# A gated delta rule whose transposes move to VectorE, with part of the output projection issued in its last slot

## The reference

```python
x = x + L0_attn(layernorm(x))            # x: 4 x 512 x 512; gated delta rule, 16 key heads, 32 value heads of 128
x = x + L0_xattn(layernorm(x), ctx, ctx) # 4 heads of 128, all of it dense
x = x + L0_ffn(layernorm(x))             # 512 -> 1280 -> 512, ternary weights

# L0_attn
mixed = silu(causal_conv1d(h @ w_qkv)); z = h @ w_z
q, k = l2norm(q), l2norm(k); beta = sigmoid(h @ w_b); g = -exp(A_log) * softplus(h @ w_a + dt_bias)
for t: S = S * exp(g_t); S += k_t (x) (v_t - k_t S) * beta_t; o_t = q_t S
core = rmsnorm(core) * norm_weight * silu(z)
return core.reshape(B, S, 4096) @ w_out
```

## Time and profile before

| | |
|---|---|
| median of 3 runs | 3666.68 us (3666.51 to 3670.01) |
| the profiled execution | 3667.28 us, of which its span 3665.5 us |
| PE busy | 3487.7 us (95%) |
| DVE busy | 2314.8 us (63%) |
| ACT busy | 1369.4 us (37%) |
| POOL busy | 1520.7 us (41%) |
| mean granted PE clock | 0.977 |
| largest group | L618, the projection tiles, 1424.5 us of PE |

### The profile page before, as it was taken

The page is one execution under the profiler, slowest core; times in us unless marked ns, Lnnn a source line. Parts: engine busy times, 40 slices in busy tenths (PEclk is TensorE's granted clock), DMA queues, the critical chain, the costliest instruction groups (busy, mean ns, idle before and its releaser), DMA issues. The chain is left out here.

```text
span 3665.5 us, 67720 instructions
## 1 busy us (share of the span) xinstructions
PE 3487.7 (95%) x23472; PEld 2207.6 (60%) x23472; DVE 2314.8 (63%) x4006; ACT 1369.4 (37%) x4187; POOL 1520.7 (41%) x1473
## 2 busy tenths in 40 slices
PE   4799999999999999999999999999996999999999
PEld 4466666666666666666666666666664444455444
DVE  4587777877778777878778777778772000014453
ACT  1344444444444444444444444444441000011232
POOL 0455554555545455555554555545551000001032
PEclk7999999999999999999999999999997999999999
DMA  1111111111111111111121111111104232311001
GB/s 55 44 36 30 42 42 37 30 36 44 34 36 30 36 32 51 30 36 36 31 48 30 36 30 41 43 37 30 36 24 157 87 115 69 103 58 69 1 9 38
DMA packets 94404, 165.88 MB, mean 45 GB/s; under 512 B 7841, under 2 KB 40737, under 8 KB 92449
## 3 DMA queue, kind: packets, MB, share of 16 engines
q1 hardware_dynamic: 93440, 152.47, 14.4%
q10 hardware_dynamic: 576, 8.39, 0.6%
HBM read 122.83 MB, written 38.01 MB: 44 GB/s over the span
## 5 line engine op out<-in xcount | busy, mean ns | idle before, releaser
L618 PE MATMUL d_ring<-xT,d_w 128*128 128x512 f32 x3072 | 1424.5, 607 | 12.0 <-DMA d_w<-in_w 11.6
L618 PEld LDWEIGHTS d_ring<-xT,d_w 128*128 128x128 f32 x3072 | 574.7, 194 | 585.6 <-issue 567.2
L890 DVE SCALAR_TENSOR_TENSOR d_conv<-d_ring,d_w,d_conv 128x511 f32<-128x511 f32 (+2 forms) x768 | 570.7, 743 | 287.2 <-ACT d_conv L1082 282.4
L1384 PE MATMUL t_acc<-t_area 128*128 128x512 f32 x1024 | 444.8, 595 | 18.4 <-DMA t_area<-core_rows 18.4
L1082 ACT ACTIVATE d_conv<-d_ring,d_w 128x512 f32<-128x512 f32 x256 | 176.5, 689 | 599.3 <-PE d_ring L618 599.3
L1384 PEld LDWEIGHTS t_acc<-t_area 128*128 128x128 f32 x1024 | 194.5, 191 | 256.7 <-issue 237.9
L923 DVE TENSOR_TENSOR d_zm<-d_tz,cons 128x512 f16<-128x512 f32 x384 | 264.2, 688 | 118.9 <-PE d_tz L688 114.5
L559 POOL TENSOR_TENSOR d_imd<-cons,d_dm 128x512 f16<-128x512 f32 x128 | 148.4, 1160 | 434.5 <-ACT d_dm L1133 434.5
L1613 DVE TENSOR_TENSOR t_x<-t_acc,t_x 128x512 f32<-128x512 f32 x16 | 11.1, 692 | 419.5 <-PE t_acc L1384 419.5
L511 POOL TENSOR_TENSOR d_rkt<-d_kss,cons 128x4 f32<-128x4 f32 x64 | 12.9, 201 | 610.9 <-ACT d_junk L1100 610.9
L933 DVE TENSOR_TENSOR d_em<-d_te,d_em 128x512 f16<-128x512 f32 x384 | 262.1, 683 | 4.5 <-PE d_td L697 0.2
(11 more groups left out here) (223 smaller groups left out, 6791.1 us busy)
## 6 DMA issues: line engine op xcount, KB each, us to landing
d_decay<-decay_rows SPq DMA_DIRECT2D x64, 512.0 KB, 6.1
core_rows<-d_core SPq DMA_DIRECT2D x64, 512.0 KB, 3.3
t_area<-core_rows SPq DMA_DIRECT2D x32, 1024.0 KB, 5.5
d_w<-in_w SPq DMA_DIRECT2D x96, 256.0 KB, 2.8
t_area<-in_wout ACTq DMA_DIRECT2D x2, 3072.0 KB, 21.3
ln_x<-in_x SPq DMA_DIRECT2D x16, 256.0 KB, 5.1
t_x<-in_x SPq DMA_DIRECT2D x4, 1024.0 KB, 9.9
t_area<-in_ctx SPq DMA_DIRECT2D x4, 1024.0 KB, 7.5
```

What stands on the lines that cost most here:

```text
L618: last = nc.tensor.matmul(bank(TILE[j])[:, :], wtile(j, k), xT[:, k, r % B * S:(r % B + 1) * S], start=k == 0, stop=k == KT - 1)
L890: nc.vector.scalar_tensor_tensor(c[:, d:S], bank(TILE[j])[:, 0:S - d], tap(j, KS - 1 - d), c[:, d:S], ALU.mult, ALU.add).then_inc(taps, 1)
L1384: return nc.tensor.matmul(acc[t][:, :], core[(grp * CHUNKS + q) % 3][:, t, h * P:(h + 1) * P], w[:, head, :], start=head == 0, stop=head = ...
```

## The change

1. Levels 0 to 3 no longer compute E on PE. DVE turns D into E by one instruction, `nc.vector.transpose` of 128 x 1024 fp16 in blocks of 32x32, after each of the levels 0 to 3 (`flip_d`), and E into the first D at the start (`flip_e0`). `turn_e0` and `copy_d0` go; `level_e` stays at levels 4 and 5.
2. `normal_k` moves from DVE to ACT (four instructions instead of one). `p_full` moves from DVE to POOL and reads a copy that ACT makes (`copy_kq`). The two copies of chunk 0 move from DVE to ACT (`first_state`, `first_output`).
3. The orders of all engines in a slot, the ring's order and banks, and the lags are new. v1's tile now comes after v0's.
4. `xT` and four PSUM banks `acc` (the ring and `td`) live on through `tail`. SP loads the core rows of heads 0 to 7 for group 0, and `w_out` of these heads, into columns of `xT` that are no longer needed. PE issues 24 of the 32 products on them in 19 places of the last slot and the other 8 at the start of `tail`; the output projection then starts at chunk 2. The loads of core rows and weights in `tail` are cut and ordered anew.

```diff
+EARLY = 24
@@ SP
+            sp.wait_ge(z_projected, GV * (ITERS - 1))
+            sp.wait_ge(stored, 16 * (ITERS - 4))
+            for q, b in ((0, 1), (1, 0)):
+                sp.dma_start(xT[:, :, b * S:(b + 1) * S], core_rows[0:NC, :, q * S:(q + 1) * S].rearrange("t p n -> p t n")).then_inc(early[0], 16)
+            sp.dma_start(xT[:, :, 2 * S:3 * S], wout[:, 0:KT, :]).then_inc(early[0], 16)
             slot((ROUNDS, 0), False, True, True)
+            sp.wait_ge(z_projected, GV * ITERS)
+            sp.dma_start(xT[:, :, 3 * S:4 * S], wout[:, KT:2 * KT, :]).then_inc(early[1], 16)
             slot((ROUNDS, 1), False, False, True)
@@ POOL
+            def p_full(m, h):
+                pool.wait_ge(kqs_ready, count(m))
+                pool.wait_ge(gamc_ready, nth(m, "gamc_ready", h))
+                nc.gpsimd.tensor_tensor(pT[m[1] % 2][h][:, :], kqs[:, :], gamc[m[1] % 2][h][:, :], ALU.mult).then_inc(p_ready, 1)
@@ PE
-            def turn_e0(m, h):
...
             def level_d(m, l):
                 pe.wait_ge(z_ready, at(m, LEVELS, l + 1))
-                if l:
-                    pe.wait_ge(e_added, at(m, LEVELS, l))
+                elif l < 5:
+                    pe.wait_ge(flipped, at(m, 5, l + 1))
...
+            def head_start(n, i):
+                if isinstance(n[0], int) and n == (ROUNDS, 1):
+                    if i == 0:
+                        pe.wait_ge(early[0], 48)
+                        pe.wait_ge(vn_ready, GV * ITERS)
+                        pe.wait_ge(z_silued, GV * ITERS)
+                        pe.wait_ge(zr_ready, GV * ITERS)
+                    for piece in range(EARLY * i // 19, EARLY * (i + 1) // 19):
+                        if piece == 4 * KT:
+                            pe.wait_ge(early[1], 16)
+                        early_product(nc, acc, xT, piece)
@@ DVE
+            def flip_e0(m):
+                dve.wait_ge(e0_ready, at(m, 2 * GV, 2 * GV))
+                nc.vector.transpose(dm[:, :], em[m[1] % 2][:, :]).then_inc(flipped, 1)
+
+            def flip_d(m, l):
+                dve.wait_ge(d_added, at(m, 4, l + 1))
+                nc.vector.transpose(em[m[1] % 2][:, :], dm[:, :]).then_inc(flipped, 1)
@@ ACT
+            def normal_k(n):
...
+                for c in range(NC):
+                    nc.scalar.activation(chunk(khat[n[1] % 2], c), chunk(bank("k_turn"), c), ACT.Copy, scale=rk[:, c:c + 1]).then_inc(khat_ready, 1)
+            def copy_kq(m):
...
+                nc.scalar.activation(kqs[:, :], bank("kq")[:, :], ACT.Copy).then_inc(kqs_ready, 1)
+            def first_state(s):
+                act.wait_ge(s_done, at(s, 3, 1))
+                nc.scalar.activation(state[:, :], psa[:, 0:GV * P], ACT.Copy).then_inc(first_ready, 1)
+            def first_output(s):
+                act.wait_ge(o_done, at(s, NC, 1))
+                nc.scalar.activation(oo[:, :, 0, :], psb[:, 0:GV * P].rearrange("p (h d) -> p h d", h=GV), ACT.Copy).then_inc(first_ready, 1)
@@ tail
+def early_product(nc, acc, xT, piece):
+    head, t = piece // 4, piece % 4
+    core = xT[:, t, (1 - head // 4) * S + head % 4 * P:(1 - head // 4) * S + (head % 4 + 1) * P]
+    return nc.tensor.matmul(acc[t][:, :], core, early_weights(xT, head), start=head == 0, stop=False)
-        PARTS = (0, 2, 8, 20, HV)
+        PARTS = (8, 12, 16, 24, HV)
...
+            for piece in range(EARLY, 8 * KT):
+                early_product(nc, acc, xT, piece)
             for grp in range(B):
-                for q in range(CHUNKS - 2):
+                for q in range(0 if grp else 2, CHUNKS - 2):
...
             for i in range(4):
+                if i:
+                    act.wait_ge(core_loaded[i - 1], 16)
                 act.dma_start(w[:, PARTS[i]:PARTS[i + 1], :], a["wout"][:, PARTS[i]:PARTS[i + 1], :]).then_inc(w_loaded[i], 16)
```

More of the change, by code:

```diff
@@ L424, in conv_of, with free @@
             return cb[CONV_BUFFER[name]]
-        def free(eng, n, name, order, place, freed):
-            slot_, v = back(n, -(name in LAGGED)), order.index(name)
+        def free(eng, n, name, order, place, freed, lag):
+            slot_, v = back(n, -lag[name]), order.index(name)
             for _ in range(3 * len(order)):
@@ L666, in _ @@
             PIECES = [(h, c) for h in range(GV) for c in range(NC)]
-            def turn_e0(m, h):
[L669 to L676, removed]
-                    last = nc.tensor.matmul(chunk((tz, td)[h], c), piece(em[m[1] % 2], h, c), id16[:, :], start=True, stop=True)
-                last.then_inc(a_done, 1)
             def level_z(m, l):
                 if l == 0:
-                    pe.wait_ge(d0_ready, at(m, GV, GV))
+                    pe.wait_ge(flipped, at(m, 5, 1))
+                    wait(pe, tt_ready, nth(m, "tt_ready", 1, 1))
                 elif l < 5:
@@ L822, in slot @@
                 if recur:
-                    solve(s, 2)
-                if invert:
-                    level_e(m, 2)
-                if recur:
-                    read_q(s, 2)
+                    attend(s, 1)
+                    head_start(n, 7)
+                    read_k(s, 2)
+                    head_start(n, 8)
+                if project:
+                    khat_turn(n)
                 if invert:
@@ L847, in slot @@
                 if recur:
-                    solve(s, 3)
-                if project:
-                    kk(n)
+                    attend(s, 2)
+                    head_start(n, 12)
+                    read_k(s, 3)
+                    head_start(n, 13)
                 if invert:
@@ L871, in slot @@
                 if recur:
+                    solve(s, 3)
+                    head_start(n, 15)
+                if invert:
+                    level_z(m, 5)
+                    v_turn(m, 1)
+                if recur:
+                    attend(s, 3)
+                    head_start(n, 16)
+                if invert:
+                    level_d(m, 5)
+                    level_e(m, 5)
+                if project:
+                    tile(n, 3)
+                if invert:
+                    refine(m, 1)
+                    refine(m, 0)
+                    tile(m, 4)
+                    close(m, 0)
+                if recur:
+                    o_turn(s, 0)
+                    head_start(n, 17)
                     o_turn(s, 1)
+                    head_start(n, 18)
                 if invert:
-                    close(m, 0)
                     close(m, 1)
+                    v_turn(m, 0)
             slots(pe, slot)
@@ L1110, in q_square @@
                 wait(act, eq_ready, count(n, 1))
-                squares(bank("q_turn"), NC, qss, q_squares, scale=(RMS_EPS * HD) ** 0.5)
+                wait(act, k_squares, at(n, NC, NC))
+                squares(bank("q_turn"), 0, qss, q_squares, scale=(RMS_EPS * HD) ** 0.5)
             def copy_kT(n):
```

445 lines of the change are left out of this document (222 added, 223 removed).

## The result

The changed kernel takes 3542.18 us in the median of four runs (3536.55 to 3546.47), beside 3667.24 us for the kernel before: a ratio of 0.9657, with an interval of 0.9640 to 0.9673. It is 3.4% faster, 125 us. The forecast was 3567 us with a range down to 3545, so the sign and the cause are as forecast, and the gain is 25 us larger than forecast and 3 us larger than the range allowed. The profiled execution is the slowest of the four, 3546.47 us, with a span of 3544.6 us.

What follows compares the result with a forecast made beforehand. PE was taken to bound the delta rule. From 3667.28 us: -86.8 for PE work removed, +9 for waits, -1.3 for slot 1, -21 at the end, giving 3567 us; range 3545 to 3612.

Steps and rivals of the forecast that it cites:

- The bound: Delta rule: PE is the bound, its groups following without a gap, so only work taken from PE shortens the 40.14 us slot.
- Together 1.40 us of PE in a slot: Four `level_e` (0.95 us) and two unit-matrix turns (0.46) leave PE; slot 38.74 us, 86.8 us less over 62 slots.
- The unknown price: One DVE 32x32 block transpose of 128 x 1024 fp16, shown in no row: taken as 1.21 us, bounds 0.68 and 2.66.
- The booked waits: PE's waits at six tight places in a slot: 0.15 us a slot, 9 us in all, between 0 and 0.6 a slot.
- The draining slots and slot 1: Slots without all three parts: slot 1 gives 1.3 us, the first draining slot 0, within 2 us either way.
- The end: Last slot and tail: +12 for early products, -27.8 for 32 products gone, -5 for an earlier tail start; sum -21 us.
- The turns: Hardware loop's turn of a round: PE waits 3.3 us, 12 times, taken as the loop's price and left as is.
- the lists don't mesh: Rival, chance 0.20: several tight places short by 0.3 or more, 0.5 to 1.0 us a slot lost, 3590 to 3620 us.
- DVE becomes the bound: Rival, chance 0.07: transposes at the scan's pace make DVE set the slot, 3780 us; decides from 2.2 us a transpose.
- The slots did shorten: Answers a rival, chance 0.05: POOL or ACT paces the slot at 40 us, only the end's -21 is left, 3646 us.
- the end did give: Answers a rival without its own chance: early products at half clock throughout, +21 us in the last slot, 3588 us.

Runs made afterwards that it cites:

- The first two experiments: Changed kernel plus 32 unread PE products a slot, in four groups of eight: behind each level's `level_d`, 3599.12 us; between fp32 groups, 3627.16 us.
- the second experiment: Changed kernel plus four groups of eight unread fp16 products on PE, each standing between fp32 groups: 3627.16 us, ratio 0.9902.
- the fourth experiment: Changed kernel with the DVE transposes (`flip_d`) of levels 0 to 3 each done twice: 3670.66 us, ratio 1.0022 to the kernel before.

## Why the prediction was near, and where it was short

**The bound.** Right: PE was the bound in the delta rule and still is, and what left PE's list left the slot. The first two experiments show it by putting it back.

**The slot: the step that failed.** "Together 1.40 us of PE in a slot" was too small: what left PE's list was worth 1.60 (fp16 groups 1.38, the fp32 groups behind them 0.22). I took the durations of the removed groups, 0.24 and 0.23, but put at nothing what they did to the fp32 groups behind them. Such a group takes up to 0.08 us longer behind fp16, and the second experiment makes four such places and pays 0.08 for each. Summed by distances between starts in a regular slot of either kernel:

| us of a slot | before | after |
|---|---|---|
| fp32 groups, each as long as behind fp32 | 32.93 | 32.93 |
| fp16 groups | 6.02 | 4.64 |
| what fp32 groups take longer behind fp16 | 1.18 (16 places) | 0.96 (15 places) |
| late starts at `level_d` 4 and `attend` 3 | 0 | 0.10 |
| sum | 40.13 | 38.63 |

The new order has one such place less, and at four of them instead of one it is a turn that stands there, which takes 0.01 or 0.03 us longer instead of 0.08. So 1.38 + 0.22 = 1.60 us left PE, 0.10 came as late starts, and the slot fell by 1.50. Over 62 slots the mis-sized term is 12 us, the largest part of the miss.

**The unknown price.** Right: 1.240 us against 1.21. DVE's share came out at 85 to 86% (forecast 85), POOL's at 61 to 63 (64), ACT's at 53 to 55 (55).

**The booked waits.** "I book 0.15 us of waits for a slot, 62 x 0.15 = 9 us, between 0 (all latencies met) and 0.6". What came is 0.10 at most, 6 us, and none of it as idle time in a row. Of the two places that I had short by 0.05 and 0.06, v1's tile shows no delay and `level_d` 5 one of 0.01; the 0.10 stands at two places that I had with no room or with 0.05. That the sum is near is luck as far as the places go. At `level_z` 1, the place that an experiment tried, there was no room: a sum that starts 0.39 us later costs 0.37.

**The draining slots and slot 1.** Booked at 1.3 in sum, within 2. The last two distances between first solves went from 38.27 and 33.07 to 37.68 and 31.19 us, 2.5 less, with a little from the other turns and slots. The whole miss ahead of the last slot is 17.8 us: 12.4 of the removed work, 2.8 of waits, 2.6 here.

**The end.** The booking for the last slot was +12; from the first `solve` to the end of the last early product it was 23.3 us and is 36.1, +12.8. 32 products less, 27.8, held. The start of the tail was booked at -5 and is about -10: PE passes into the next block 1.93 us after its last product, where I took the 4.1 us of before, the eight products took 8.6 instead of 9.5 us, and the loads that I had arriving 2 us behind them were there. Against this, some 1 us is lost further on. In all 24.0 us instead of 21.

**The turns.** I took the turn as one unchanged price and read it as a 3.3 us wait. The whole price is the round less four slots, 6.1 us before. That it stayed nearly unchanged (85.0 and 83.2 us in all) is luck, since PE's stall got shorter and DVE's longer. The changed kernel's four runs are spread over 10 us, and those in rounds of 16 over 3, so the turns probably vary from run to run; no trace of the faster runs shows it.

**The range.** From the forecast's 3567.2 for the profiled execution the measured terms lead to its 3546.5: 17.8 us ahead of the last slot and 3.0 at the end. The range's lower end was 3555 (the terms give 3554) and 10 us for cheaper turns, and had nothing for more work leaving PE than was counted. The median is 4.3 us below the profiled execution, and this was enough to take a result of 3546.5, inside the range, to 3542.2, outside it.

**The rivals.** Of "the lists don't mesh" 0.10 us a slot came, where it had 0.5 to 1.0. The condition of "DVE becomes the bound" did not hold, and the fourth experiment puts its point earlier than I had it. The slots did shorten, and the end did give.

## What to carry to other kernels

Where one engine is dense and the trace shows no gap, price a removed instruction by the distance between starts and price its neighbour as well. Where waits are looked for, compare the distance between two starts with that of the same group elsewhere, since a short delay shows as no idle time. Before tuning inside a loop, subtract the pitch of a slot from the round: here the remainder was 83 us, and longer rounds gave back 72 of them by changing one number. And look at the turn in the lists of all engines: DVE's stall of 4.4 us did not stand in PE's rows by name.

## What the runs showed of the hardware

- A DVE block transpose of 128x1024 fp16 takes 1.24 us, one element in 1.2 ns for each partition.
- An fp32 matmul group of four products 128x128 or of a tile behind an fp16 one of 64 columns takes 0.08 us longer than behind an fp32 one, a group of fp32 turns 0.03 longer.
- A PE wait in a row can be 0.2 us less than what the work behind it loses, because the records ahead are still draining: 0.19 us in the row, 0.36 lost.
- At the loop turns of the changed kernel PE stood 2.0 to 2.5 us; behind eight of the 14 stalls the granted clock was 0.57 to 0.67 over the next 4 us, behind six it was full. In rounds of 8 a turn with half clock cost 3.8 to 4.0 us and one with full clock 2.1 or 2.4.
- The turn of a loop costs 5.9 to 6.1 us in rounds of 4 slots and 3.6 in rounds of 8.
- At each turn of the changed kernel in rounds of 4 DVE stood a second time, 3.7 to 5.3 us (`issue`), and at none in rounds of 8 and 16, with the same instructions in a slot.
